# Flamingo block with a mixture of experts: moving the last group's normalisation between POOL, ACT and DVE slots

## What is computed

```
x = x + tanh(g_xattn) * attention(ctx, layernorm(x), mask, ...)
xf = layernorm(x).reshape(4096, 128)
probs = softmax(xf @ router_w.T)            # 8 experts
topv, topi = top_k(probs, 2); topv /= topv.sum() + 1e-9
h = gelu(einsum('td,edh->teh', xf, w1))     # 128 -> 512
y = einsum('teh,ehd->ted', h, w2)           # 512 -> 128
x = x + tanh(g_ffn) * sum over the two chosen experts of topv * y
```

## Time and profile before

| | before |
|---|---|
| median of 3 runs | 332.65 us (332.07 to 334.12) |
| profiled execution, time | 334.15 us |
| profiled execution, span of the trace | 332.3 us |
| mean granted TensorE clock | 0.97 |

### The profile page before, as it was taken

How to read it: one execution, slowest core, us unless ns; L and a number is a source line. 1 busy time by engine, 2 the same in 40 slices (tenths; PEclk the granted TensorE clock), 3 DMA queues, 4 the chain that set the end, 5 groups by cost and what they waited for, 6 DMA issues and landing times.

```text
span 332.3 us, 10883 instructions
## 1 busy us (share of the span) xinstructions
PE 296.3 (89%) x3521; PEld 266.6 (80%) x3521; DVE 219.0 (66%) x909; ACT 194.0 (58%) x502; POOL 220.5 (66%) x301
## 2 busy tenths in 40 slices
PE   8789999999998999896888979999998999999920
PEld 3668788787876878785668969999998999999920
DVE  2776567689899998889568796435853433434653
ACT  3466869888795877856575427547444444444300
POOL 3735455354787888888455878778877876555860
PEclk9997999999999999999799997999999999999995
DMA  6643522202151211850134222311352432229346
GB/s 215 183 120 126 186 71 70 63 22 92 52 128 34 68 50 49 248 146 26 54 98 112 66 67 72 91 50 57 98 128 82 137 108 78 68 72 352 102 134 189
DMA packets 41237, 34.60 MB, mean 104 GB/s; under 512 B 5045, under 2 KB 36951, under 8 KB 41185
## 3 DMA queue, kind: packets, MB, share of 16 engines
q1 hardware_dynamic: 32608, 23.10, 24.8%
q0 software_dynamic: 4320, 8.47, 7.2%
q10 hardware_dynamic: 4256, 2.36, 2.4%
HBM read 22.35 MB, written 12.01 MB: 103 GB/s over the span
## 4 chain that ended last, share of the span: by engine, by line
PE 44%; POOL 22%; issue 16%; DVE 8%; ACT 5%; DMA 3%; POOLq 0%; SPq 0%; ACTq 0%; DVEq 0%
POOL rows L653 10%; PE ps_sc L1596 9%; POOL picked L671 8%; PE ps_proj L1609 4%; PE ps_o L1609 4%; PE ps_o L1555 3%; PE ps_proj L1490 3%; PE ps_proj L1493 3%; PE ps_sc L1439 3%; PE ps_sc L1434 2%; PE ps_proj L1501 2%; PE ps_o L1475 2%; ACT xr L801 2%; DVE rowmax L1225 2%; PE ps_proj L1502 2%
## 5 line engine op out<-in xcount | busy, mean ns | idle before, releaser
L671 POOL DMA_INDIRECT picked<-yo,xg x71 | 71.6, 1008 | 16.3 <-issue 11.6
L1596 PE MATMUL ps_sc<-xt,w1c 128*128 128x128 f32 x568 | 76.2, 278 | 3.2 <-issue 2.4
L653 POOL DMA_INDIRECT rows<-xr,posi x64 | 63.1, 985 | 18.0 <-issue 18.0
L1596 PEld LDWEIGHTS ps_sc<-xt,w1c 128*128 128x128 f32 x568 | 69.8, 193 | 4.2 <-issue 4.1
L835 ACT ACTIVATE probT<-ps_sc 128x512 f32<-128x512 f32 x71 | 42.4, 598 | 43.5 <-PE ps_sc L1596 42.6
L724 ACT ACTIVATE probT<-ps_sc,pencol 128x512 f32<-128x512 f32 x64 | 43.6, 683 | 23.4 <-PE ps_sc L1453 13.1
L1225 DVE TENSOR_REDUCE rowmax<-ps_sc 128x4 f32<-128x512 f32 x64 | 43.7, 685 | 15.5 <-PE ps_sc L1453 13.2
L591 POOL TENSOR_TENSOR kblkr<-kT,headcol 128x256 fp32r<-128x256 f32 x32 | 19.7, 616 | 39.1 <-ACT kT L761 38.8
L1609 PE MATMUL ps_proj<-w2s,probT 128*128 x288 | 38.9, 279 | 0.0
L1609 PE MATMUL ps_o<-w2s,probT 128*128 x280 | 37.1, 275 | 0.0
L1345 DVE COPY w1c<-w1s 128x512 f32 x71 | 31.6, 449 | 7.0 <-PE ps_sc L1596 2.3
(11 more groups left out here) (169 smaller groups left out, 618.0 us busy)
## 6 DMA issues: line engine op xcount, KB each, us to landing
xg<-rows SPq DMA_DIRECT2D x71, 65.0 KB, 1.8
ctxs<-ctxT SPq DMA_DIRECT2D x32, 128.0 KB, 2.4
xs<-x SPq DMA_DIRECT2D x8, 256.0 KB, 3.0
maskbc<-mask SPq DMA_DIRECT2D x8, 256.0 KB, 4.7
w1s<-w SPq DMA_DIRECT2D x4, 512.0 KB, 3.8
w2s<-w SPq DMA_DIRECT2D x8, 256.0 KB, 4.8
maskbc<-picked SPq DMA_DIRECT2D x4, 512.0 KB, 6.5
out<-xs ACTq DMA_DIRECT2D x6, 256.0 KB, 2.3
```

The costliest lines, as they stand in the source:

```text
L653: nc.gpsimd.indirect_dma_start(out=rows, out_offset=bass.IndirectOffsetOnAxis(ap=posi[:, i, pick, b:b + 1], axis=0), in_=xr[:, i, pick, b, ...
L671: nc.gpsimd.indirect_dma_start(out=picked, out_offset=bass.IndirectOffsetOnAxis(ap=xg[:, r, D + 1:D + 2].bitcast(I32), axis=0), in_=yo[:, ...
L1596: last = nc.tensor.matmul(ps_score[j % DEEP][:, c * 128:(c + 1) * 128], w1c[:, j % DEEP, c * 128:(c + 1) * 128], xt[:, j % XRING, :], star ...
```

## The change

Four edits, all in the mixed stretch. `AHEAD` = (10, 2) names the step; `slot_at(10, 2)` is 12, so `slot_at(*AHEAD) - 3` is slot 9.

- POOL makes the factors of group 7 in slot 9, behind the scatters of that slot and ahead of its sends, no longer in step (10,2) between the slots 11 and 12.
- ACT makes the four normalisations of group 7 one by one at the ends of the slots 14, 15, 16 and 17, no longer together in step (10,3) between the slots 14 and 15.
- DVE makes the w1 copy first in every slot, ahead of positions and plan pieces.
- The middle plan's `carry` is cut into the two sums (`sum_open`) and the rest, and the pieces now lie in the slots 6, 7, 8, 9, 10, 11, 13 and 14: slot 12 has none.

```diff
+AHEAD = (10, 2)
+MIDDLE_AT = (6, 7, 8, 9, 10, 11, 13, 14)
...
 # POOL, step
-                if k == 2 and G is not None:
-                    pool.wait_ge(s_ln2, G + 1)
...
+                if k == 2 and G is not None and (g, k) != AHEAD:
+                    factors(G)
...
 # POOL, slot
                     if 0 <= t < 2 * GROUP:
                         scatter(G, (t, t + 1))
+                if n == slot_at(*AHEAD) - 3:
+                    factors(AHEAD[0] - LAG_OUT)
                 j = slot_of(n, LAG_DOWN)
...
+            def factors(G):
+
+                pool.wait_ge(s_ln2, G + 1)
+                wait(pool, s_x2n, GROUP * G)
+                nc.gpsimd.tensor_tensor(rs2[:, :], ve2[:, :], minus_half[:, :],
+                                        ALU.pow).then_inc(s_rs2, 1)
+                pool.wait_ge(s_rs2, G + 1)
+                pool.wait_ge(s_nm2, G + 1)
+                nc.gpsimd.tensor_tensor(mr2[:, :], nm2[:, :], rs2[:, :], ALU.mult).then_inc(s_mr2, 1)
...
 # ACT, step
-                if k == 3 and G is not None:
...
+                if k == 3 and G is not None and g != AHEAD[0]:
+                    normalise_again(G, range(GROUP))
...
 # ACT, end of slot
+                b = n - slot_at(*AHEAD) - 2
+                if 0 <= b < GROUP:
+                    normalise_again(AHEAD[0] - LAG_OUT, (b,))
...
+            def normalise_again(G, seqs_of):
+
+                box, used = outbox(G)
+                act.wait_ge(s_mr2, G + 1)
+                act.wait_ge(s_x2, G + 1)
+                wait(act, s_send[box], SEND * used)
+                for b in seqs_of:
+                    nc.scalar.activation(
+                        xr[:, box, 0, b, 0:D], xs[:, bass.ds(GROUP * G + b, 1), :].rearrange("p o d -> p (o d)"),
+                        ACT.Identity, bias=mr2[:, b:b + 1], scale=rs2[:, b:b + 1]).then_inc(s_x2n, 1)
...
 # DVE, plan
+                def sum_open():
+                    sums(last, stop, 2, late_exp, late_row)
+
                 def carry():
                     count = stop - last
-                    sums(last, stop, 2, late_exp, late_row)
...
 # DVE, slot
             def slot(n):
+                j = slot_of(n, 0)
+                if j is not None:
+                    if j % REGS == 0:
+                        turn["experts"] = experts_of(mybir.EngineType.DVE, j, min(REGS, SLOTS - j))
+                    wait(dve, f_up, j - DEEP + 1)
+                    nc.vector.tensor_copy(
+                        w1c[:, j % DEEP, :],
+                        w1s[:, turn["experts"][j % REGS], :].rearrange("p o h -> p (o h)")).then_inc(f_w1, 1)
                 for G in range(GROUPS):
...
-                    late_pieces.update(enumerate(middle_plan(), n))
+                    late_pieces.update(zip(MIDDLE_AT, middle_plan()))
...
                 if n in late_pieces:
                     late_pieces[n]()
-                j = slot_of(n, 0)
...
```

More of the change, by code:

```diff
@@ L1189, in carry @@
                     assert planned[0] == CARRIED
-                return count_full, end_full, pass_ends, write, end_open, pass_open, carry
+                return count_full, end_full, pass_ends, write, end_open, pass_open, sum_open, carry
             def last_plan():
```

## The result

The changed kernel is slower: 337.15 us median of 4 runs (336.75 to 337.66) beside 333.26 us (332.07 to 334.12, also 4 runs by then), a ratio of 1.0118 with a 95% interval of 1.009 to 1.0145. The forecast was 334.0 us in a range up to 335.8. The profiled execution took 337.66 us, its span is 335.8 us, 3.5 us more than before.

A forecast was written before the change was run, and what follows sets the result against it. POOL's full queue was taken to set slot 41's start, so PE's 2.8 us lead becomes waiting and the slow clock costs 1.3 us: 332.65 + 1.3 = 333.95, say 334.0 us, range 330.6 to 335.8.

The forecast's parts named there:

- What bounds the end: Slot 41: POOL's always full queue, 70 us of DMAs, sets when tile 41 loads; PE waits 0.98 us.
- PE's gain becomes a wait at slot 41: Slot 41: PE comes about 2.8 us sooner but starts at 255.6 as before, so it waits 3.8 us.
- rival C: Slot 9: POOL's factors wait for DVE's `ve`, cover 0.35 us; 2.55 us on top of the forecast, 336.5 us; chance 0.10.
- the normalisations need no other activation table: ACT, slots 14 to 17: single normalisations among the Gelus cost 0.41 us each and 0 for table loads.
- the price of the clock: Behind slot 41: the longer wait drops PE's granted clock to 0.50 for 3.4 us, costing 1.3 us, between 0 and 1.7.
- 332.65: Starting time of the kernel before: the median of the runs, 1.5 us below the profiled execution of 334.15 us.
- POOL's queue is as long as before: POOL up to the load of tile 41: scatter, landing and load at the old times, slot 41 at 255.6.
- Moving copies ahead elsewhere adds nothing to DVE's sum: DVE, the other slots: w1 copies placed first cost nothing; each waits for a PE matmul long done.
- Rival B: POOL's queue: stretched DMAs go, at most 2.05 us, PE keeps its clock at slot 41; 330.6 us, chance 0.13.
- DVE's edits were told as what frees PE: Slots 14 to 18: the w1 copy no longer behind `carry` ends PE's stall; 2.8 us recovered, bounds 2.0 and 4.3.
- POOL's and ACT's as free of cost: Factors in slot 9: zero for the chain; single normalisations: 0 for tables, 0.15 us of wait inside the 2.8 us.

The follow-up runs named there:

- the filled wait: The changed kernel with 18 extra bf16 128x512 matmuls on PE ahead of the transpose of tile 41, output untouched: 334.11 us, ratio 1.0002 to the kernel before.
- copy behind: The changed kernel with the w1 copy back behind positions and plan pieces in each slot, all else as changed: 335.58 us, ratio 1.0041 to the kernel before.

## Why the prediction was wrong

**Right, and shown by the runs.** What bounds the end: the kernel with POOL's queue lengthened is later by the addition and more, the two kernels with the last scatter moved up lose their wait. That PE's gain becomes a wait at slot 41: 4.71 us before the load, with 2.6 us won in the slots 14 to 18 where I had put 2.8. That no wait of POOL for its factors arises (rival C, whose 336.5 us came nearest to the measured time for a reason that was not there): `ve` was ready 2.1 us ahead of them, and POOL's and ACT's parts alone make no difference. That the normalisations need no other activation table: each takes 0.48 to 0.50 us in the profile after (I had put 0.41), with no table load but those around the Exp.

**The step that failed** is the price of the clock in the sum: "I take 1.3 us; the ends are 0 (no fall) and 1.7 (the whole 3.4 us on work)". Both falls that I had read lasted 3.4 us, and I took that for the length of any fall. Behind slot 41 the clock stayed low for 6.83 us, twice as long, and 5.42 us of it met work: 2.7 us. The kernel with the filled wait won that back, 2.6 us in its trace and 3.0 us between the medians. The start of the fall was close: 3.3 us into the wait (251.89 to 255.19), where I had read 2.65 and 3.25. Why this fall lasted longer stays open; two rows of one execution could not show that the length changes, as the last section tells.

The clock alone does not put the result out of the range: 332.65 + 2.7 is 335.35 us, and the range ended at 335.8. Two more terms do.

**A term that was put at nothing:** "POOL's queue is as long as before", so slot 41 starts "at 255.6 as before". It started at 256.60. I had counted the copies in front as free ("Moving copies ahead elsewhere adds nothing to DVE's sum"), but POOL's queue got 0.8 us longer with the whole change (72.9 against 72.1 us), which on a full queue goes to slot 41 whole. Rival B had the thought with the other sign, and its counter-argument, that stretched operations only change places, was wrong. With 0.8 for the queue and 2.7 for the clock the sum is 332.65 + 3.5 = 336.15.

**What no step explains:** the median of the kernel before was 333.26 us with its fourth run, 0.6 us above the 332.65 that I started from; its runs lie between 332.07 and 334.12. From there the sum is 336.8, and 0.4 us to the 337.15 are left open.

**A chance that doesn't follow:** I called 330.6 the most that rival B could reach, and put a quarter of it below 329.3 all the same. Nothing measured hangs on it.

**A side that was misjudged:** DVE's edits were told as what frees PE, POOL's and ACT's as free of cost. Each part alone gives no gain on PE from slot 14 to slot 18 (14.23 and 12.89 us, before 12.62); together they take 10.05 us.

## What to carry to other kernels

Before an engine is sped up, follow the chain back from the last start that everything waits for: if another engine's queue sets that start, the gain becomes a wait, and on PE the wait can cost a slow stretch behind it: here 2.6 us won became 4.71 us of wait, and 2.6 us were lost behind it. Do not take the length of a slow stretch from one or two examples. The cheap remedy was in the order of the queue that binds: four sends moved behind the scatters for which SP waits, no work removed, took the ratio from 1.0118 to 0.9866. With them the same edits on DVE, POOL and ACT were worth 0.7%.

## What the runs showed of the hardware that was not expected

The length of a fall of the granted clock to 0.50 is not fixed, and the idle time before it does not say it. At slot 41 it was 6.8 us behind waits of 3.03, 3.51 and 4.71 us, and none in one execution behind 2.74 us; with DVE's part alone 3.78 us of idle time in slot 17 brought 3.4 us. The plainest case is the idle stretch of 2.19 us at about 157 us, which stands in all twelve profiled executions. Behind it the clock was low for 3.4 us in seven of them (the kernel before and the changed one among them), for 6.8 us in two and for 10.2 us in three. One of the two (copy behind) and one of the three (the kernel before with the scatters sooner):

```profile
156.14 0.30 PE L1486 MATMUL ps_xT<-ident,rowmax 128*128 128x128 f32 x1 [2.19 <-DVE rowmax L1244]
```
```profile
157.31:164.12 6.81, 6.81 (x77) 5.12 (x75) 3.08 (x9) 3.39 (x7) 2.99 (x4) 0.50 0.18 53
```
```profile
157.37 0.45 PE L1467 MATMUL ps_xT<-ident,rowmax 128*128 128x128 f32 x1 [2.19 <-DVE rowmax L1225]
```
```profile
156.72:166.94 10.22, 9.57 (x100) 7.79 (x104) 4.52 (x18) 4.90 (x11) 3.99 (x5) 0.50 0.22 61
```

From the end of that stretch to slot 14 it is 37.7 to 37.9 us where the fall lasted 3.4 us, 38.5 and 38.7 us with 6.8, and 39.4 to 39.7 us with 10.2. The kernel before and the same with the scatters sooner are the same code up to slot 14, and they differ there by 1.8 us (37.9 and 39.7) with the length of the fall. The two executions with the scatters sooner differ by 2.1 us (37.7 and 39.7), most of the 2.2 us between them at slot 14. What decides the length in a given execution these runs do not settle.

POOL's queue of some 70 us got 0.8 us longer with nothing added to it: single POOL operations take longer where they run beside an operation on DVE, a w1 copy above all. POOL and DVE of the changed kernel in order of time:

```profile
204.40 0.41 POOL L674 TENSOR_TENSOR pscratch<-minus_half 1x1 f32<-1x1 f32 x1
204.96 1.25 POOL L679 DMA_INDIRECT picked<-yo,xg  x1 [0.16 <-POOL pscratch L674]
```
```profile
204.34 0.43 DVE L1351 COPY w1c<-w1s 128x512 f32 x1 [0.20 <-issue]
...
204.94 0.42 DVE L1351 COPY w1c<-w1s 128x512 f32 x1
```

The carrier takes 0.18 us and the send 0.98 us where no copy starts with them. In this stretch of the changed kernel five carriers take 0.36 us or more; each of them starts at most 0.1 us behind the start of a w1 copy and ends within 0.05 us of the copy's end. With the copy behind, no carrier of the stretch takes more than 0.30 us. Sends and scatters don't stretch beside every copy: nine of this stretch of the changed kernel have a copy beside them in their first 0.15 us and take 1.03 us or less. The scatters, which make 0.3 us of the difference to the kernel before, met another operation: the longest of them, 1.25 us, and one of 1.08 us run beside `gone`, a subtraction of a plan piece, and not beside a copy. The longest and what DVE did:

```profile
192.32 1.25 POOL L661 DMA_INDIRECT rows<-xr,posi  x1 [0.30 <-issue]
```
```profile
192.08 0.66 DVE L1121 TENSOR_TENSOR gone<-past,hops 128x480 f32<-128x480 f32 x1
```

The Trainium skill, "SBUF — State Buffer", section "SBUF: two separate sides", says that of a GpSimd operation and a DVE copy of this kind the one that starts first holds the port that they share until it ends, and the other waits; the carrier, which ends with its copy (204.81 against 204.77), agrees with that, and the send lost 0.27 us beside a copy of 0.42 us.
